# Moving a preparation product ahead of a state product, and an output update behind an inner update, in the loop of a gated delta rule

## The reference

```python
def step(S, xs):
    q_t, k_t, v_t, g_t, b_t = xs
    S = S * jnp.exp(g_t)[..., None, None]
    kv = jnp.einsum('bhk,bhkv->bhv', k_t, S)
    S = S + jnp.einsum('bhk,bhv->bhkv', k_t, (v_t - kv) * b_t[..., None])
    o_t = jnp.einsum('bhk,bhkv->bhv', q_t, S)
    return (S, o_t)
```

## Time and profile before

| | |
|---|---|
| median of 3 executions | 4097.55 us (4093.26 to 4102.58) |
| profiled execution | 4104.73 us, its span 4103.0 us |
| TensorE busy | 3673.0 us, 90% of the span |
| VectorE busy | 2470.9 us, 60% |
| ScalarE busy | 1540.4 us, 38% |
| GpSimd busy | 883.9 us, 22% |
| VectorE's `whole_level` (L3352) | 512 instructions, 205.0 us busy, 214.2 us idle before them, 203.1 of it waiting for TensorE's L2947 |
| granted clock of TensorE, mean | 0.957 |

### The profile page before, as it was taken

The page is one execution under the profiler, slowest core; times in us unless marked ns, Lnnn a source line. Parts: engine busy times, 40 slices in busy tenths (PEclk is TensorE's granted clock), DMA queues, the critical chain, the costliest instruction groups (busy, mean ns, idle before and its releaser), DMA issues. The chain is left out here.

```text
span 4103.0 us, 93379 instructions
## 1 busy us (share of the span) xinstructions
PE 3673.0 (90%) x37500; PEld 2356.3 (57%) x37500; DVE 2470.9 (60%) x5994; ACT 1540.4 (38%) x3558; POOL 883.9 (22%) x1564
## 2 busy tenths in 40 slices
PE   6998999988898889999979989999888988999999
PEld 3886886433354336665548868864333544466655
DVE  6677676566435676555466676765665356765454
ACT  4445444233222335432244454432332222345322
POOL 1441441011001203320024414410110011133100
PEclk9999999999999999899989999999999999989999
DMA  2000000010000000010010000000100000000100
GB/s 95 3 3 2 3 3 13 1 54 1 21 1 20 1 25 2 1 41 18 12 35 3 3 1 3 3 13 1 54 1 21 1 20 1 26 1 1 41 29 6
DMA packets 8676, 59.92 MB, mean 15 GB/s; under 512 B 893, under 2 KB 5297, under 8 KB 5937
## 3 DMA queue, kind: packets, MB, share of 16 engines
q1 hardware_dynamic: 8240, 53.86, 3.4%
HBM read 52.81 MB, written 1.05 MB: 13 GB/s over the span
## 5 line engine op out<-in xcount | busy, mean ns | idle before, releaser
L97 PE MATMUL psum<-ident_bf 128*128 128x512 bf16 x1304 | 323.2, 393 | 15.3 <-PEq L2566 4.0
L3113 ACT ACTIVATE l_attn_ax<-psum 128x128 f32<-128x128 f32 (+1 forms) x768 | 186.4, 278 | 397.0 <-PE psum L2928 276.8
L3352 DVE TENSOR_TENSOR l_attn_xx<-l_attn_xx,psum 128x256 f32<-128x256 f32 x512 | 205.0, 419 | 214.2 <-PE psum L2947 203.1
L438 ACT ACTIVATE l_ffn_silu<-psum 128x512 f32<-128x512 f32 (+2 forms) x208 | 124.1, 597 | 469.5 <-PE psum L404 415.0
L503 DVE TENSOR_TENSOR l_ffn_hidden<-l_ffn_silu,psum 128x512 f32<-128x512 f32 (+2 forms) x176 | 120.5, 687 | 283.6 <-ACT l_ffn_silu L438 283.6
L103 PEld LDWEIGHTS psum<-streamed_weights,l_ffn_hidden 128*128 128x128 f32 (+2 forms) x1664 | 215.4, 192 | 123.0 <-issue 112.3
L2943 PE MATMUL psum<-l_attn_ax,l_attn_xx 64*64 64x64 f32 x5120 | 272.0, 226 | 0.0
L2947 PE MATMUL psum<-l_attn_xx,l_attn_ax 64*64 64x64 f32 x5120 | 263.9, 223 | 0.0
L3239 POOL TENSOR_TENSOR l_attn_part<-l_attn_ab,streamed_weights 128x128 f32<-128x128 f32 x640 | 245.4, 414 | 39.4 <-PE psum L2928 20.3
L103 PE MATMUL psum<-streamed_weights,l_ffn_hidden 128*128 128x128 f32 (+2 forms) x1664 | 224.2, 278 | 14.1 <-DVE l_ffn_hidden L503 9.2
L97 PEld LDWEIGHTS psum<-ident_bf 128*128 128x128 bf16 x1304 | 126.3, 103 | 183.0 <-issue 50.1
(11 more groups left out here) (541 smaller groups left out, 7858.7 us busy)
## 6 DMA issues: line engine op xcount, KB each, us to landing
streamed_weights<-pack_l_ffn SPq DMA_DIRECT2D x2, 5284.0 KB, 15.3
streamed_weights<-pack_l_attn SPq DMA_DIRECT2D x3, 2848.5 KB, 9.6
streamed_weights<-pack_l_ffn SPq DMA_DIRECT2D x2, 3972.0 KB, 13.0
streamed_weights<-pack_l_xattn SPq DMA_DIRECT2D x2, 2496.0 KB, 9.4
streamed_weights<-pack_l_ffn SPq DMA_DIRECT2D x2, 2192.0 KB, 8.1
streamed_weights<-pack_l_xattn SPq DMA_DIRECT2D x2, 2048.0 KB, 8.8
streamed_weights<-pack_l_ffn SPq DMA_DIRECT2D x2, 1923.0 KB, 7.9
streamed_weights<-pack_l_attn SPq DMA_DIRECT2D x2, 1091.5 KB, 5.1
```

What stands on the lines that cost most here:

```text
L97: pe.matmul(self.bank(bank), self.ident_bf[:, :], self.ident_bf[:, :].unsqueeze(1).to_broadcast([P, NT, P]), start=True, stop=True)
L3113: act.activation(ax[b, p, :, :], m.psum[b, p, 0:P].rearrange("p (i t) -> p i t", i=2), ACT.Copy).then_inc(ax_ready, 1)
L3352: dve.tensor_tensor(both, both, m.psum[:, p, P:384], ALU.subtract).then_inc(x_less, 1)
```

## The change

Three things are written in another order; no arithmetic, tile or size is touched.

1. On TensorE `prep` of the FIRST pairs for step n + 2 is issued in level 6 of step n, in front of `add` of the SECOND pairs. It was issued in level 1 of step n + 1, behind `whole_level`. Only `prep(1, FIRST)` stays in level 1 of step 0.
2. `m.side.turn`, which needs bank 4 free, goes from level 1 of step 6 to level 6 of step 6, also in front of `add`; ScalarE's copy of it goes to level 6 of step 6, and the wait for that copy to level 1 of step 7.
3. On VectorE `output` of the FIRST pairs is issued behind `whole_level` of level 3 instead of in front of it.

```diff
@@ TensorE
                         if n < STEPS:
                             half_level(n, l)
-                        if n == 6 and l == 1:
-                            m.side.turn(pe, [m.psum[:, 4, t * P:(t + 1) * P] for t in range(NT)])
                         if l == 1:
                             past(n, ks, FIRST)
...
                         if n < STEPS:
                             whole_level(n, l)
-                        if n == 6 and l == 1:
-                            m.side.taken(pe)
-                        if l == 1:
-                            coming(n, prep, FIRST)
+                        if l == 1 and n == 0:
+                            prep(1, FIRST)
                         elif l == 3:
                             coming(n, turn, FIRST)
...
                         elif l == 6:
+                            if n + 2 < STEPS:
+                                prep(n + 2, FIRST)
+                            elif n == STEPS - 2:
+                                pe.wait_ge(x0_ready, UNITS)
+                                m.side.turn(pe, [m.psum[:, 4, t * P:(t + 1) * P] for t in range(NT)])
                             past(n, add, SECOND)
                         if n == STEPS - 1 and l == 1:
+                            m.side.taken(pe)
                             gate(0, 0)
@@ ScalarE
-                        if n == 6 and l == 1:
+                        if n == STEPS - 2 and l == L:
                             m.side.copy(act, m.bank(4))
@@ VectorE
-                        if last and l == 3:
-                            output(n - 1, FIRST)
                         if last and l == 4:
                             add(n - 1, FIRST)
                         if last and l == 6:
                             output(n - 1, SECOND)
                         if n < STEPS and l < L:
                             whole_level(n, l)
+                        if last and l == 3:
+                            output(n - 1, FIRST)
```

## The result

The changed kernel takes 4053.15 us (median of 4 executions, 4044.77 to 4062.58), the kernel before 4100.07 beside it: ratio 0.9887, 95% interval 0.9859 to 0.9916. I had predicted 4054.5 and a ratio of 0.9895. Timed again in two further series, it gave 0.9887 (0.9867 to 0.9908) and 0.9870 (0.9853 to 0.9887). The profiled execution has a span of 4060.9 us against 4103.0.

What follows compares the result with a forecast made beforehand. TensorE was taken to set the loop's pace, with only its waits and clock to be won. 20 + 15 + 8 = 43 us off the 4097.55 us median gave 4054.5 us, ratio 0.9895; range 4040 to 4062.

Steps and rivals of the forecast that it cites:

- The stalls: Ends of steps 2 to 5: preparation fills TensorE's 16 waits for `output`, 20.8 us together; 20 us taken.
- The cover in level 1: Without the preparation there, VectorE's level 1 updates still reach level 2's first product in time, the last by 0.33 us.
- the rival with 0.08: TensorE's wait moves into level 1 or 2, giving 4080 to 4090 us; chance 0.08.
- the slower rival: Clock also falls at ends of steps 1, 2, 3 and 6: 14 us slower, 4111.5 us; chance 0.03.
- the rival without a change: `output` follows TensorE's progress, so a later state product only shifts the wait: no change; chance 0.03.
- The clock: Half-clock stretches after steps 4 and 5 vanish: 3.9 us a run, 15.7 in four; 15 us taken, bounds 0 and 26.
- The sentence on which it rested: In this trace the clock falls after steps 4 and 5 follow TensorE stalls of 1.4 and 1.1 us.
- The rival with 0.25: The clock keeps falling, or falls elsewhere for as long: only 28 us gained, 4069.5 us; chance 0.25.
- Step 0: Clock fall after step 0: counted as 0; its recovery, 10.5 us more, only an upper bound.
- The third edit: Level 4, steps 1 to 7: VectorE's updates earlier, last pair 0.30 us sooner; 8 us taken, bounds 0 and 10.9.
- the sum: First layer's attention loop: waits 20, clock 15 and level 3 update order 8, together 43 us.

Runs made afterwards that it cites:

- the norm's parts: Kernel before, with VectorE's parts of the other sequence's norm moved from level 5 to level 1 in steps 2 to 5: 4060.5 us, ratio 0.9896.
- The dummies alone: Kernel before, with three dummy 128x512 bf16 matmuls in front of the state's product in steps 2 to 5, nothing moved: 4076.8 us, ratio 0.9939.
- the third profile of the same kernel: The changed kernel, unaltered, timed and profiled a third time beside the preparation's move alone: 4050.8 us, loop 839.8 us.
- run 1: First of the four runs per execution (two passes, two sequences each) of the first layer's attention loop; not a separate kernel or experiment.
- run 2: Second of the four runs per execution (two passes, two sequences each) of the first layer's attention loop; not a separate kernel or experiment.
- the kernel with the later scores: Changed kernel with norm parts in level 1, plus VectorE's scores product (`pm`) of second pairs issued behind level 5's `turn`: 4036.7 us, ratio 0.9843.
- the three comparisons: Loops without and with VectorE's level 3 update ahead of `output`: preparation moved, 848.1 and 847.9 against changed kernel's 838.97 and 839.8; dummy matmuls, 875.0 against 865.3 us.

## Why the prediction was right

**The stalls.** 20 us taken of the 20.8 in the earlier trace rows; all 16 waits are gone. Shown by the pair of experiments that put the preparation in front of the state's product and behind it (0.9887 and 1.0003, both with the third edit), and by the norm's parts, whose move alone removes the same waits.

**The cover in level 1.** Predicted: every update in time. In the changed kernel level 2's first product starts 0.23 us behind level 1's last (215.46 to 215.69), runs 1.14 us, and has no wait. So the wait did not move there (the rival with 0.08); neither did new half-clock stretches come behind steps 1, 2, 3 or 6 (the slower rival), nor did `output` follow TensorE (the rival without a change): VectorE finished it early and waited itself.

**The clock.** 15 us taken. The dummies alone took 15.5 us off the loop in like runs, so the size was right. The sentence on which it rested, that stalls of 1.1 and 1.4 us bring the fall, is shown by that run: the same place, the same waits for the output, more matmuls in them, and no fall. The norm's parts show it once more without a dummy. But the stall alone doesn't decide: in the kernel before, those of 1.59 and 1.07 us at the ends of steps 2 and 3 bring no fall. The rival with 0.25 falls, and with it here the Trainium skill's rule ("TensorE: Matmul & The Clock Gate", section "HAM oscillation — how this bites in real kernels"), by which waits this short leave the clock alone. Which steps the fall hits was less fixed than I thought: it takes 0.26 us less in a step to move it from two steps to three.

**Step 0.** I counted nothing there, as nothing in front of its fall is changed. In two of the four runs it is gone (clock 1.00 above), in the third profile of the same kernel in runs 1 and 4; run 1 is 2.9 us longer with it (210.92 against 207.99). The waits in front of it are short. In the kernel before, run 1, with the stretch behind them:

```profile
121.08 0.44 PE L2924 MATMUL psum<-l_attn_xx,l_attn_ab 64*64 64x64 f32 x4 [0.37 <-DVE l_attn_solved L3359]
121.89 1.18 PE L2924 MATMUL psum<-l_attn_xx,l_attn_ab 64*64 64x64 f32 x5 [0.37 <-DVE l_attn_solved L3359]
121.90:125.30 3.40, 3.27 (x47) 3.08 (x49) 1.84 (x7) 1.73 (x8) 1.05 (x3) 0.50 0.02 5
```

The same place in run 2 of the changed kernel has the same waits (0.24 us, then 0.37 each) and no fall:

```profile
436.40:439.80 3.40, 3.40 (x54) 2.60 (x54) 0.60 (x3) 1.57 (x8) 0.88 (x2) 1.00 0.00 0
```

The fall comes and goes within one kernel, and the kernel with the later scores has it in all four runs; I take it to hang on the moment at which the loop is entered, which wasn't tried by itself.

**The third edit.** 8 us taken; the loops of the three comparisons differ by 9.1, 8.1 and 9.7, but each has one fall behind step 0 more on the side without the edit. By the runs that match, 7, 6 and 7.5 are left, so the term was about 1 us too large. The step was right, but not what I said it would look like: level 4's first product did not get down to 1.2 us, since its first pairs start earlier too. From L2850 to L2907 it is 1.89 us instead of 197.48 - 195.34 = 2.14; before:

```profile
195.34 0.63 PE L2850 MATMUL psum<-streamed_weights,l_attn_part 64*64 64x64 f32 x16
```

In the whole kernel's time the gain is plausible, not shown.

**What the sum missed.** 43 us were predicted for the loop and 54 came. The step with no stall, 29.03 us by the prediction's reckoning, takes 236.24 - 207.48 = 28.76 us with the preparation's move alone, although the same matmuls are issued. The place matters. In level 1 the preparation made 217.39 - 215.36 = 2.03 us between the products around it, and 215.69 - 215.46 = 0.23 are left: 1.80 us. In level 6 it costs less. Without it, in step 6 of the kernel before:

```profile
304.96 1.01 PE L2938 MATMUL psum<-l_attn_solved,l_attn_ax 64*64 64x64 f32 x13
306.03 0.60 PE L2907 MATMUL psum<-l_attn_u_end,l_attn_k 128*64 128x128 f32 x4
306.56 0.33 PE L2928 MATMUL psum<-l_attn_xx,l_attn_part 64*64 64x64 f32 x4
```

From L2938 to L2928 these are 1.60 us; with it, 211.97 - 208.97 = 3.00: 1.40 us. Step 3 of the kernel with the norm's parts in level 1, which lacks the preparation there too, gives 210.09 - 208.48 = 1.61. Of the 0.40 us a step, 0.27 show in the length of step 4; the loop's runs that match in step 0's fall are 42.1 us shorter in four with the move alone, of which 20.8 and 15.5 are stalls and clock, so some 6 are left for the place. I had moved the preparation at an unchanged price. The 54 us are then 20.8 + 15.5 + 7 and 6 for the place, and some 5 for the two falls behind step 0 that are gone. That the median came out within 1.4 us of the forecast is partly luck: the loop gave 11 us more than the sum, one term was 1 us too large, and the median is of only four executions. Over three series the changed kernel was 46.9, 45.8 and 53.8 us faster, not 43.

## What to carry to other kernels

When an engine waits in a fixed place for another one's queue, look at what stands in that queue ahead of the instruction it waits for, and at what of its own it could do meanwhile. Either cure took the whole stall here, both together no more. And price the clock with the stall: three useless matmuls in a wait made this kernel 25 us faster, and shortening each step by 0.26 us with the stalls left in made it no faster at all. Where single executions spread by 10 us, compare the loop's own length in the profiles too, and only between runs with equally many falls of the clock: one fall more or less made the third edit look 2 us better than it is.

## What was not expected of the hardware

- The clock fell after TensorE waits of 1.07 to 1.6 us in a loop where it was otherwise busy, and which steps it hit shifted with the length of a step: behind two steps of run 1 in the kernel before (10.2 us at 1.2 GHz), behind three with the third edit alone (13.6 us), behind none of steps 2 to 5 with 0.8 us of dummies in each wait. Behind step 0 it fell in some runs and not in others after waits of no more than 0.37 us.
- Small matmuls of two groups, each 64x64, start mixed: at the end of step 3 the first of L2938 starts at 208.75, 0.01 us behind one of L2924 and ahead of that line's next at 208.84, although the program lists all of L2924 first.
- The same four preparation matmuls cost 1.80 us between 64x64 products and 1.40 us in front of the state's product. Whether it is that the state's product also reads 128 partitions of weights, like the preparation's first matmuls, was not tried by itself.
